# Attention outputs split to 16 bits by a constant instead of by their norm, and a PSUM bank moved from the work ring to the score ring

## What is computed

```
qkv = layernorm(x) @ Wqkv.T + b          # 16 query heads, 8 key heads of 128; 4 value groups of 256
p1, p2 = softmax(causal(q1 k1')), softmax(causal(q2 k2'))     # a pair of heads makes one output
p = p1 - lam * p2
o = p @ v                                # 256 channels
o = o * rsqrt(mean(o*o) + EPS) * subln_w * (1 - LAMBDA_INIT)
y = concat(o over 8 outputs) @ out_w.T + out_b
x = x + layernorm(y)
x = x + layernorm(ffn(layernorm(x)))     # Hadamard, silu(gate) * up, Hadamard, down
```

## Time and profile before

| | |
|---|---|
| median of 3 runs | 1268.17 us (1265.16 to 1270.18) |
| the profiled execution | 1270.65 us, span of its instructions 1268.8 us |
| mean granted TensorE clock | 0.991 |
| busy: PE, DVE, ACT, POOL | 1202.4, 1021.7, 997.8, 780.3 us |
| chain that ended last | PE 56%, DVE 17%, POOL 8%, issue 6%, ACT 5%, DMA 5% |

### The profile page before, as it was taken

The page is one execution under the profiler, slowest core; times in us unless marked ns, Lnnn a source line. Parts: engine busy times, 40 slices in busy tenths (PEclk is TensorE's granted clock), DMA queues, the critical chain, the costliest instruction groups (busy, mean ns, idle before and its releaser), DMA issues.

```text
span 1268.8 us, 26516 instructions
## 1 busy us (share of the span) xinstructions
PE 1202.4 (95%) x8102; PEld 1011.7 (80%) x8102; DVE 1021.7 (81%) x2620; ACT 997.8 (79%) x2607; POOL 780.3 (62%) x1045
## 2 busy tenths in 40 slices
PE   7899999999999999999899999999998898999998
PEld 6788788888878888788788888788876787777887
DVE  6888988888779898988688888778788998846545
ACT  4799889988689989988688888887887898856341
POOL 3576666655657675646476575455567986776532
PEclk9999999999999999999999999999998998999999
DMA  3245554563266555534655554534563555540001
GB/s 130 65 78 103 88 97 93 93 103 71 45 122 105 88 95 90 107 58 64 121 86 91 88 96 85 101 55 82 117 105 86 90 99 94 97 88 1 29 18 38
DMA packets 368154, 106.62 MB, mean 84 GB/s; under 512 B 359312, under 2 KB 365712, under 8 KB 367504
## 3 DMA queue, kind: packets, MB, share of 16 engines
q1 hardware_dynamic: 366672, 103.37, 44.8%
q10 hardware_dynamic: 1344, 1.57, 0.4%
HBM read 14.71 MB, written 2.10 MB: 13 GB/s over the span
## 4 chain that ended last, share of the span: by engine, by line
PE 56%; DVE 17%; POOL 8%; issue 6%; ACT 5%; DMA 5%; SPq 1%; ACTq 0%; POOLq 0%; DVEq 0%
PE score_bank L1039 7%; PE score_bank L1173 6%; PE score_bank L1045 6%; PE score_bank L1042 6%; DVE p L1453 5%; DVE mx L1442 4%; POOL e_all L1736 3%; PE turn_bank L1066 3%; PE turn_bank L1067 3%; PE turn_bank L1068 3%; DMA oT<-o 3%; ACT e_all L1212 2%; DMA p16T<-p 2%; DVE score_bank L1437 2%; PE turn_bank L1119 2%
## 5 line engine op out<-in xcount | busy, mean ns | idle before, releaser
L1212 ACT ACTIVATE e_all<-score_bank,negmx 128x512 f32<-128x512 f32 (+2 forms) x640 | 393.6, 623 | 52.4 <-DVE negmx L1446 36.8
L1736 POOL TENSOR_TENSOR e_all<-e_all 128x512 f32<-128x512 f32 (+3 forms) x320 | 367.8, 1162 | 40.4 <-ACT e_all L1227 30.5
L1039 PE MATMUL score_bank<-k_hi,q_hi 128*128 128x512 f32 (+2 forms) x640 | 255.9, 400 | 27.8 <-ACT e_all L1212 15.5
L1453 DVE SCALAR_TENSOR_TENSOR p<-e_all,gain,p 128x512 f16<-128x512 f32 (+3 forms) x320 | 261.2, 831 | 11.3 <-ACT p L1234 10.5
L1442 DVE TENSOR_REDUCE mx<-score_bank 128x1 f32<-128x512 f32 (+1 forms) x384 | 242.1, 638 | 26.2 <-PE score_bank L1045 25.4
L1042 PE MATMUL score_bank<-k_lo,q_hi 128*128 128x512 f32 (+2 forms) x640 | 232.4, 363 | 0.4 <-DVE k_lo L1503 0.4
L1045 PE MATMUL score_bank<-k_hi,q_lo 128*128 128x512 f32 (+2 forms) x640 | 232.5, 363 | 0.0
L1234 ACT ACTIVATE p<-e_all,gain 128x512 f16<-128x512 f32 (+3 forms) x320 | 204.2, 666 | 20.4 <-POOL e_all L1736 19.7
L1781 POOL TENSOR_SCALAR ratio<-s,inv,neg_lam 128x1 f32<-128x1 f32 x128 | 55.9, 437 | 256.1 <-DVE inv L1724 255.8
L1039 PEld LDWEIGHTS score_bank<-k_hi,q_hi 128*128 128x128 f32 x640 | 121.3, 189 | 66.4 <-issue 27.5
L1066 PE MATMUL turn_bank<-v,p16T 128*128 128x256 f16 x567 | 157.1, 277 | 3.4 <-DVE o L1483 1.3
(11 more groups left out here) (391 smaller groups left out, 2789.0 us busy)
## 6 DMA issues: line engine op xcount, KB each, us to landing
p16T<-p SPq DMA_TRANSPOSE x320, 3.1
w_raw<-in_w_qkv_dram SPq DMA_DIRECT2D x3, 1024.0 KB, 5.4
w_raw<-in_w_o_dram SPq DMA_DIRECT2D x4, 512.0 KB, 3.3
oT<-o SPq DMA_TRANSPOSE x128, 2.5
bv<-in_hidden_dram SPq DMA_DIRECT2D x8, 256.0 KB, 3.0
w_raw<-in_w_ug_dram SPq DMA_DIRECT2D x4, 512.0 KB, 4.0
out_dram<-e SPq DMA_DIRECT2D x16, 128.0 KB, 1.7
e<-in_w_d_dram SPq DMA_DIRECT2D x1, 1024.0 KB, 6.2
```

The costliest lines, as they stand in the source:

```text
L1039: pe.matmul(bank[:, 0:w], qh, kh, start=True, stop=False)
L1212: act.activation(e, S[k % NS][:, 0:w], ACT.Exp, bias=negmx[:, d % 2, m, s:s + 1], scale=-1.0 if alone else 1.0, accum_out=ssum[:, d % 4, s ...
L1453: dve.scalar_tensor_tensor(out=halves_of(q, w)[1], in0=e1_of(q, w), scalar=gain[:, d % 4, s:s + 1], in1=halves_of(q, w)[0], op0=ALU.mult, ...
L1736: pool.tensor_tensor(a, a, b, ALU.add).then_inc(p_pool, 1)
```

## The change

Three things change together.

- `OH` and `OL` scale the output by the constant `O_SHRINK` = 2^-15 and no longer by `rms`. The norm's factor goes into the accumulation `OP` on DVE (L1535), whose column is now `rms` of this output in place of the group's `out_unit`.
- `VE` on DVE is gone. Its addition, together with a multiplication by the (now squared) `out_unit` of the group, is a new instruction on POOL in `norm`, ahead of pow, so that `rms` holds the whole factor. POOL waits there for the square, and for the accumulation four outputs back, since `rms` is held until then. `OS`, once for each of four groups, has one instruction more.
- `NS` becomes 5 and `WORK_BANKS` 3: one turn_bank leaves the work ring and a fifth score bank comes. The planner's costs and conditions of these steps change with it (`OT` 0.55 to 0.85 and rank 1, `OH` 0.37 to 0.28 and free to start with `SQ`), so all engines' orders are planned anew.

```diff
--- before.py
+++ after.py
@@ -33,7 +33,7 @@
 DUOS = TILES
 ALL_DUOS = GROUPS * DUOS
 CHUNKS = 5
-NS = 4
+NS = 5
 WORK_BANKS = 8 - NS
 E1_ROOM = 10 * BANK
 E2_ROOM = 7 * BANK
@@ -42,6 +42,7 @@
 
 HALF_MAX = 32768.0
 O_UNIT = 2048.0
+O_SHRINK = 2.0 ** -15
 
 MASKED = -1e30
 LOWEST = -3e38
@@ -221,14 +222,14 @@
         elif kind == "PV":
             o, last = duo_chunks(what[0])[what[1]][0], duo_chunks(what[0])[what[1]][5]
             if last:
-                add("P", "ACT", "SQ", o, 0.37, [pe] + ([("DVE", "VE", o - 4)] if o >= 4 else []), 0)
-                add("N", "DVE", "VE", o, 0.13, [("ACT", "SQ", o)], 0)
-                add("N", "POOL", "OT", o, 0.55, [("DVE", "VE", o)] + ([("DVE", "OL", o - 4)] if o >= 4 else []), 0)
-                add("R", "ACT", "OH", o, 0.37, [("POOL", "OT", o)] + ([("SP", "OX", o - 4)] if o >= 4 else []), 0)
+                add("P", "ACT", "SQ", o, 0.37, [pe] + ([("POOL", "OT", o - 4)] if o >= 4 else []), 0)
+                add("P", "ACT", "OH", o, 0.28, [pe] + ([("SP", "OX", o - 4)] if o >= 4 else []), 0)
+                scaled = [("POOL", "OS", o // (2 * DUOS))] if o % (2 * DUOS) == 0 else []
+                add("N", "POOL", "OT", o, 0.85, [("ACT", "SQ", o)] + scaled + ([("DVE", "OP", o - 4)] if o >= 4 else []), 1)
                 add("R", "DVE", "OL", o, 0.4, [("ACT", "OH", o)], 0)
                 add("X", "SP", "OX", o, 1.2, [("DVE", "OL", o)] + ([("PE", "OP", o - 4)] if o >= 4 else []), 0, 2.2)
         elif kind == "OP":
-            add("Q", "DVE", "OP", what, 0.4, [pe], 1)
+            add("Q", "DVE", "OP", what, 0.4, [pe, ("POOL", "OT", what)], 1)
             if what % (2 * DUOS) >= 2 * DUOS - 2 and what // (2 * DUOS) + 1 < GROUPS:
                 steps_of("WO", (what // (2 * DUOS) + 1, next(ch[1] for ch in duo_chunks(what // 2) if ch[0] == what)))
             tile = next(ch[2] for ch in duo_chunks(what // 2) if ch[0] == what)
@@ -609,7 +610,7 @@
 
         whole.enter_context(nc.allow_non_contiguous_dma(reason="short columns of biases and scales"))
         S = [whole.enter_context(nc.psum_tensor(f"score_bank{b}", [P, BANK], F32)) for b in range(NS)]
-        T = [whole.enter_context(nc.psum_tensor(f"turn_bank{b}", [P, BANK], F32)) for b in range(2)]
+        T = [whole.enter_context(nc.psum_tensor(f"turn_bank{b}", [P, BANK], F32)) for b in range(WORK_BANKS - 2)]
         O = whole.enter_context(nc.psum_tensor("sum_bank", [P, BANK], F32))
         R = whole.enter_context(nc.psum_tensor("proj_bank", [P, BANK], F32))
 
@@ -848,7 +850,7 @@
             scaled_by_act = {x: n for n, x in enumerate([x for k, x in orders["ACT"] if k == "E2"])}
             scaled_by_pool = {x: n for n, x in enumerate([x for k, x in orders["POOL"] if k == "E2"])}
 
-            WORK = (T[0], T[1], R, O)
+            WORK = (*T, R, O)
             latest = [(-4, None), (-3, None), (-2, None), (-1, None)][:WORK_BANKS]
             bank_of, before = {}, {}
             for n, (kind, what, *_) in enumerate(steps):
@@ -1235,20 +1237,19 @@
                                        scale=gain[:, d % 4, s:s + 1]).then_inc(p_hi, 1)
                     elif kind == "SQ":
                         o = what
-                        act.wait_ge(pv_done, max(CHUNKS * (o // 2) + j for j, ch in enumerate(duo_chunks(o // 2))
-                                                 if ch[0] == o) + 1)
+                        act.wait_ge(pv_done, last_part[o] + 1)
                         if o >= 4:
-                            act.wait_ge(rms_step, o - 3)
+                            act.wait_ge(rms_ready, o - 3)
                         act.activation(o_half[:, o % 2, :], bank_for("PV", o)[:, 0:HID], ACT.Square,
                                        scale=float(2 * D) ** -0.5 / O_UNIT, accum_out=msq[:, o % 4:o % 4 + 1])\
                            .then_inc(msq_ready, 1)
                     elif kind == "OH":
                         o = what
-                        act.wait_ge(rms_ready, o + 1)
+                        act.wait_ge(pv_done, last_part[o] + 1)
                         if o >= 4:
                             act.wait_ge(turned_o[o % 4], 16 * (o // 4))
                         act.activation(o16[:, o % 4, 0:HID], bank_for("PV", o)[:, 0:HID], ACT.Copy,
-                                       scale=rms[:, o % 4:o % 4 + 1]).then_inc(o_hi, 1)
+                                       scale=O_SHRINK).then_inc(o_hi, 1)
                     elif kind == "OQ":
                         act.wait_ge(w_landed, 16 * (2 * what + 2))
                         if what == 0:
@@ -1481,7 +1482,7 @@
                         o = what
                         dve.wait_ge(o_hi, o + 1)
                         dve.scalar_tensor_tensor(out=o16[:, o % 4, HID:2 * HID], in0=bank_for("PV", o)[:, 0:HID],
-                                                 scalar=rms[:, o % 4:o % 4 + 1], in1=o16[:, o % 4, 0:HID],
+                                                 scalar=O_SHRINK, in1=o16[:, o % 4, 0:HID],
                                                  op0=ALU.mult, op1=ALU.subtract).then_inc(o_lo, 1)
                     elif kind == "OS":
                         dve.wait_ge(o_full, what + 1)
@@ -1528,12 +1529,11 @@
                         o, u = what, r_use[kind, what]
                         _, i = tile_of(o)
                         dve.wait_ge(r_full, u + 1)
-                        if o % (2 * DUOS) == 0:
-                            dve.wait_ge(so_ready, o // (2 * DUOS) + 1)
+                        dve.wait_ge(rms_ready, o + 1)
                         dve.wait_ge(r_free, u)
                         so_far = out_b_row[:, :] if first_visit[o] else acc[:, i, :]
                         dve.scalar_tensor_tensor(out=acc[:, i, :], in0=bank_for(kind, o)[:, 0:HID],
-                                                 scalar=out_unit[:, o // (2 * DUOS):o // (2 * DUOS) + 1], in1=so_far,
+                                                 scalar=rms[:, o % 4:o % 4 + 1], in1=so_far,
                                                  op0=ALU.mult, op1=ALU.add).then_inc(r_free, 1)
                     elif kind == "LN":
                         dve.wait_ge(x_landed[what], 32 if what < 2 else 16)
@@ -1698,15 +1698,6 @@
                             finish(what - 1)
                     elif kind == "DEND":
                         finish(TILES - 1)
-                    elif kind == "VE":
-                        o = what
-                        c, g = slice(o % 4, o % 4 + 1), o // (2 * DUOS)
-                        dve.wait_ge(msq_ready, o + 1)
-                        if o % (2 * DUOS) == 0:
-                            dve.wait_ge(eps_ready, g + 1)
-                        if o >= 4:
-                            dve.wait_ge(rms_ready, o - 3)
-                        dve.tensor_scalar(rms_b[:, c], msq[:, c], eps_v[:, g:g + 1], None, ALU.add).then_inc(rms_step, 1)
                     elif kind == "SUMS":
                         o = what
                         d, chunks = o // 2, [ch for ch in duo_chunks(o // 2) if ch[0] == o]
@@ -1736,10 +1727,16 @@
                     pool.tensor_tensor(a, a, b, ALU.add).then_inc(p_pool, 1)
 
                 def norm(o):
-                    c = slice(o % 4, o % 4 + 1)
+                    c, g = slice(o % 4, o % 4 + 1), o // (2 * DUOS)
+                    pool.wait_ge(msq_ready, o + 1)
+                    if o % (2 * DUOS) == 0:
+                        pool.wait_ge(eps_ready, g + 1)
+                        pool.wait_ge(o_step, 5 * g + 5)
+                    if o >= 4:
+                        pool.wait_ge(r_free, r_use["OP", o - 4] + 1)
+                    pool.tensor_scalar(rms_b[:, c], msq[:, c], eps_v[:, g:g + 1], out_unit[:, g:g + 1], ALU.add, ALU.mult)\
+                        .then_inc(rms_step, 1)
                     pool.wait_ge(rms_step, o + 1)
-                    if o >= 4:
-                        pool.wait_ge(o_lo, o - 3)
                     pool.tensor_tensor(rms[:, c], rms_b[:, c], half_neg[:, 0:1], ALU.pow)\
                         .then_inc(rms_ready, 1)
 
@@ -1796,15 +1793,16 @@
                         pool.wait_ge(o_read, what + 1)
                         pool.tensor_scalar(o_bound[:, 1:2], o_bound[:, 0:1], 1.0, 1e-24, ALU.mult, ALU.add)\
                             .then_inc(o_step, 1)
-                        pool.wait_ge(o_step, 4 * what + 1)
+                        pool.wait_ge(o_step, 5 * what + 1)
                         pool.tensor_tensor(o_bound[:, 2:3], o_bound[:, 1:2], half_neg[:, 0:1], ALU.pow)\
                             .then_inc(o_step, 1)
-                        pool.wait_ge(o_step, 4 * what + 2)
+                        pool.wait_ge(o_step, 5 * what + 2)
                         pool.tensor_scalar(o_scale[:, g], o_bound[:, 2:3], HALF_MAX, 0.0, ALU.mult, ALU.add)\
                             .then_inc(o_step, 1)
-                        pool.tensor_scalar(out_unit[:, g], o_bound[:, 1:2], o_bound[:, 2:3], 1.0 / (HALF_MAX * O_UNIT),
```

(6 more changed lines are left out.)

1 line of the change is left out of this document (added).

## The result

| | before | after |
|---|---|---|
| median of 5 runs | 1269.82 us (1265.16 to 1272.28) | 1282.38 us (1277.84 to 1283.24) |
| the profiled execution | 1270.65 us, span 1268.8 | 1277.84 us, span 1276.0 |
| mean granted TensorE clock | 0.991 | 0.994 |

What follows compares the result with a forecast made beforehand. TensorE, busy 95% of the span, was taken as the bound, with only its gaps to win. Terms -3 + 2 - 12 - 4 + 8 + 1 = -8 us gave 1260.2 us, range 1239 to 1284.

Steps and rivals of the forecast that it cites:

- the fifth score bank: Score matmuls: waits for a free score bank shrink, between -23 (order unchanged) and 0 (planner spends it); -12 us taken.
- Release of the bank: End of each output: without DVE's step and pow in the chain, its work bank comes free 2.0 us sooner.
- The norm's work, -3: DVE loses its add and ACT's high half gets shorter; counts from 960 to 1100 us, -3 us (0 to -5).
- POOL's instruction, +2: Norm on POOL: the added instruction is hidden except for delaying DVE's probability-chunk splits, +2 us (0 to 12).
- Output products, -4: Gaps ahead of output products: earlier low half and DMA give -6, or 0 if the planner brings products forward; -4 us.
- Three work banks, +8: PV, queries, keys, values and output products share three work banks instead of four, +8 us (-2 to +20).
- the sign named against it (over 16): Sign that the forecast is wrong: gaps ahead of work-bank matmuls over 16 us more than before.
- Start, +1: Input transposes at the start: three work banks delay one tile, +1 us (0 to 3).
- Tail, "hidden, 0": Tail: emptying a bank (0.38 + 0.48) hides behind a product of at least 1.9 us, so 0.
- the kept lead: Rival: the order stays loose, score and output terms reach -23 and -6, giving 1247 us; chance 0.17.
- The bank is spent: Rival: scores run one further ahead and wait as often, PE's gaps stay 66 us, giving 1268 us; chance 0.22.
- The work banks bind: Rival: PE waits for low halves or query splits, 16 waits of 1.9 us, giving 1282 us; chance 0.20.

Runs made afterwards that it cites:

- e4: After with its 5 score and 3 work banks, but the planner starts a score only four exponentials back; 1257.6 us, ratio 0.9923 to before.
- e7: e4's order unchanged, run on 4 score banks and 3 work banks with one bank idle; 1267.27 us, ratio 0.9994 to before.
- n4: After with only the planner's cost of the norm on POOL (`OT`) set to 0.90, so new orders; 1276.62 us, ratio 1.0062 to before.
- e14: After, planner told of 6.5 instead of seven banks in the SBUF ring of the second map's exponentials; 1276.08 us, ratio 1.0069 to before.
- e2: Before with only the bank split changed, 5 score and 3 work banks, old norm; 1306.89 us, ratio 1.0308 to before.
- e1: After with the old split, 4 score and 4 work banks, so only the norm's part is left; 1267.11 us, ratio 0.9991 to before.
- e10: Norm's part with add and multiply on DVE, 4+4 banks (1248.15 us), same order, plus one unread POOL instruction per output; 1254.77 us, ratio 0.9888 to before.
- e11: After with four down-weight steps on POOL moved ahead of the norms of the last two outputs; 1277.93 us, ratio 1.0076 to before.
- n3: After with only the planner's cost of the norm on POOL (`OT`) set to 0.84, so new orders; 1275.64 us, ratio 1.0054 to before.
- n1: Before with only the planner's cost of the high half (`OH`) set to 0.40, so new orders; 1247.19 us, ratio 0.9828 to before.
- e3: After with the norm's add and multiply as one DVE instruction again, POOL keeping pow, 5+3 banks; 1276.04 us, ratio 1.0072 to before.

## Why the prediction was wrong

The failed step is the fifth score bank: "About half: **-12** (0 to -23)". Gaps ahead of scores went from 27.8 to 29.3 us, so the term was 0 or a little above, the end of its range at which the planner spends the bank. The prediction named that rule and halved it instead of following it. e4 and e7 show what halving would have needed: an order that doesn't use the bank, which then gives 9 us. In other orders that spend it the gaps ahead of scores are 17.5 to 30.3 us, and where they are low, those ahead of PVs are higher (n4, e14).

The other terms, against what the runs showed:

- **Release of the bank**, 2.0 us sooner: 2.3. The high half 383 ns: 382 to 390. The low half was costed at no saving; without its column operand it takes 414 to 418 ns instead of 477, 128 x 0.06 = 8 us of DVE. The chain became shorter as forecast. The norm's part as a whole, of which this is one piece, goes with 1.9% where work banks are three (e2 to after) and with nothing where they are four (e1); both are new orders.
- **The norm's work, -3**: DVE has 3.5 us less from 960 to 1100 us; e1's time shows no gain from it.
- **POOL's instruction, +2**: the instruction takes 466 ns (0.44 forecast), but costs 6.6 us in e10. The step that failed is "I take the lower, since DVE has air in most of the span". The earlier trace rows spoke against it; 6.6 is the middle of the stated range, and about half of the 12 that the rule of the lock gave. The Trainium skill (SBUF — State Buffer, "SBUF: two separate sides") says that a DVE instruction with two SBUF inputs and a GpSimd one that reads SBUF shut each other out, and that the one that starts first has the ports for its whole instruction. The trace agrees: two such DVE instructions took 6.40 us under a POOL that runs without a break, against 2.71 before, and in e11 2.15, where POOL's pair was the slower one.
- **Output products, -4**: the gaps went from 11.1 to 9.2, -1.9. The planner brought them forward, the other end of that term.
- **Three work banks, +8**: PV and the other users of work banks went from 19.4 to 28.2 us, +8.8, of which the waits for a DVE instruction that empties a bank are the larger part (8.2 to 15.3, output products with them). PE's waits for low halves and query splits sum to 7.6 us, where "some 10" was named. As a sum of gaps the term was right, and the sign named against it (over 16) did not come; the one named against the score term, gaps that don't fall, did. Against e1, which has the shorter hold and four banks, it is 13.6 to 28.2, +14.6, and together with the output products +10.2.
- **Start, +1**: gaps ahead of the transposes (L1023) went from 4.9 to 5.5 us; they are part of the 8.8.
- **Tail, "hidden, 0"**: 3.9 us of wait, 0.2 before. The down products that the term was about wait 0.4 us; the wait comes from POOL's order, as e11 shows: a norm with a lower rank and one more instruction, planned ahead of work that the tail needs. What is queued behind the norm on POOL was asked for the mixes, not for the last outputs.

With these sizes the sum of gaps is 1.5 - 1.9 + 8.8 + 3.7 = +12.1, which is what the rows show. What POOL's instruction costs in after's order was not measured; if it is near e10's 6.6 us, a part of it is in these gaps. Against the forecast of gaps, -12 - 4 + 8 + 1 + 0 = -7, that is 19 more, of which 13.5 are the fifth bank. The measured 1282 still lies within the stated range, 1239 to 1284.

Of the rivals, the kept lead did not come; the Trainium skill (Perfetto Trace Analysis, "Optimization Strategy") says that a gap that repeats on the engine that should be saturated can mean too little SBUF or PSUM for the next tile. By that reading the fifth bank pays; here it paid in e4, whose order leaves it as slack, and not in after. "The bank is spent" describes the scores. "The work banks bind" has the right sign and, by its 1282, the right time, but that is luck: it took 16 waits of 1.9 us, and the rows show 9 us more ahead of work banks, in short pieces, with the fifth bank's nothing and the tail beside them.

What stays open: how much of the 1.1% belongs to this one order. The same kernel in the orders of n3 and n4 lies at 1.0054 and 1.0062. The split of the banks costs between 0.1% and 2.8% by any pair of one order from each family, and about 1.2% by the pair e1 and after. Why n1's order is so much better than before's was not settled. The planner's own end (what `plan()` reckons) tells it in part: with 4+4 banks 1078 us goes with 1247 to 1255 measured, 1085 to 1089 with 1264 to 1270; with 5+3 it foretells e2 (1128.3, 1307 measured) but not the smaller steps, as 1087.4 (after) and 1097.4 (e3) gave 1282 and 1276.

## What to carry to other kernels

When a scheduler writes the order, a buffer that it is told of can turn into a longer lead and not into fewer waits; tell it of one less than there is, and the run keeps the slack (0.7% here in an unchanged order). Price a buffer by what the order counts on: a work bank taken from an order planned for it cost 2.3%, and in an order planned without it nothing that was measured. Before a change of 1% is credited or blamed, plan the unchanged kernel anew with a cost that doesn't matter; here that moved the time by 0.0% in one case and by 1.7% in the other, and it found the best kernel.

## What the runs showed of the hardware that had not been expected

- Two DVE instructions of 128x512 with two SBUF inputs each took 6.40 us in after, where POOL ran back to back, and 2.71 in before, where it soon stood idle. In e11 POOL ran back to back as well, and the pair took 2.15, while two POOL additions beside it went from 1.44 to 2.33.
- A GpSimd instruction of 128x1 whose result nothing reads, 128 times, costs 6.6 us in a kernel in which PE is busy 96% of the span (e10), although POOL is busy only 845.1 of its 1253 us.
- Scaling by a constant in place of a column of SBUF saves 60 ns of 477 on DVE (128x256, PSUM in, float16 out). On ACT it saves 90 of 475, as forecast.
- The time of one kernel goes with its mean granted clock: before took 1271.8 us in the mean at 0.988 and 1264.3 at 0.995.
